# One transpose for both halves of the probabilities, and the gathers of the value sums moved to ScalarE's queue

## The reference

```python
xn = _layernorm(x)
q = (xn @ Wq)                       # 16 heads of 32
k, v = split(xn @ Wkv)              # 4 key/value heads of 32
scores = q k^T / sqrt(32) + alibi bias, causal mask
attn = softmax(scores)              # 2048 x 2048 per head
out = attn @ v                      # then @ Wo + bo
gate = xn @ Wg^T ; up = xn @ Wu^T   # 4096 wide, weights from 4-bit codes and block scales
inter = gelu(gate) * up
x + attention(xn) + inter @ Wd^T
```

## Time and profile before

| | |
|---|---|
| time, median of 3 runs | 1842.21 us (1841.89 to 1845.7) |
| the profiled execution | 1845.56 us, its span 1843.7 us |
| TensorE busy | 1495.3 us, 81% |
| VectorE busy | 1262.5 us, 68% |
| ScalarE busy | 996.4 us, 54% |
| GpSimd busy | 996.7 us, 54% |
| mean granted TensorE clock | 0.927 of full speed |
| DMA transposes of probabilities | 768 |
| gather DMAs | 256 |

### The profile page before, as it was taken

One profiled execution on the slowest core, in us unless ns is written; L12 is line 12 of the kernel. 1 busy time (PEld: TensorE's weight loads), 2 busy tenths in 40 slices (PEclk: granted clock), 3 DMA queues, 4 the chain that ended last, 5 costly groups with the idle time before them and its releaser, 6 DMA issues. The chain is left out here.

```text
span 1843.7 us, 29952 instructions
## 1 busy us (share of the span) xinstructions
PE 1495.3 (81%) x9281; PEld 718.2 (39%) x9281; DVE 1262.5 (68%) x2642; ACT 996.4 (54%) x2124; POOL 996.7 (54%) x670
## 2 busy tenths in 40 slices
PE   6868878778878889878878879888878888788669
PEld 5733434333333334333333434333333434333234
DVE  7747677676847677677847677576757677676556
ACT  3336556555655556555655556565645556565430
POOL 3116556475555656475545656475546556475331
PEclk9978989999899999999989999899988999998889
DMA  7777868686787768686777778685877768686766
GB/s 214 213 163 143 145 110 158 108 151 122 139 143 132 152 119 157 109 154 127 145 136 132 149 121 162 111 156 111 144 138 130 148 122 160 108 147 114 121 140 210
DMA packets 793655, 261.08 MB, mean 142 GB/s; under 512 B 745696, under 2 KB 762984, under 8 KB 792952
## 3 DMA queue, kind: packets, MB, share of 16 engines
q1 hardware_dynamic: 789176, 253.53, 72.6%
q10 hardware_dynamic: 4320, 5.64, 1.1%
HBM read 52.30 MB, written 21.89 MB: 40 GB/s over the span
## 5 line engine op out<-in xcount | busy, mean ns | idle before, releaser
L1703 POOL TENSOR_TENSOR plo<-p,phi 128x1024 f16<-128x1024 f32 (+7 forms) x384 | 614.6, 1608 | 639.7 <-DMA ptl<-plo 566.5
L1436 ACT ACTIVATE p<-s_ps,shift 128x512 f32<-128x512 f32 (+3 forms) x640 | 393.1, 619 | 226.0 <-DVE shift L1572 132.1
L1448 ACT ACTIVATE phi<-p 128x1024 f16<-128x1024 f32 (+7 forms) x384 | 308.7, 807 | 273.9 <-issue 186.8
L1330 PE MATMUL s_ps<-kst,qst 128*128 128x512 f32 (+3 forms) x640 | 360.6, 565 | 86.8 <-ACT p L1436 68.9
L1551 DVE TENSOR_REDUCE mxp<-s_ps 128x1 f32<-128x512 f32 x384 | 260.5, 682 | 144.1 <-PE s_ps L1330 143.4
L1355 PE MATMUL o_ps<-pth,vst 128*32 128x256 f16 (+1 forms) x2304 | 142.2, 313 | 204.2 <-DMA ptl<-plo 150.5
L1508 DVE TENSOR_TENSOR acc<-down_ps,acc 128x512 f32<-128x512 f32 x237 | 161.4, 681 | 95.9 <-PE down_ps L1291 94.6
L1291 PE MATMUL down_ps<-wh,ih 128*128 128x512 f16 x506 | 203.3, 402 | 24.8 <-DVE acc L1508 24.7
L1553 DVE CUSTOM_DVE_ANT_0 s_ps<-s_ps,mask_row 128x128 f32<-128x128 f32 (+3 forms) x256 | 126.3, 493 | 138.3 <-PE s_ps L1330 137.7
L1313 PE MATMUL gate_ps<-xh,wh 128*128 128x512 f16 x512 | 206.3, 403 | 0.0
L1355 PEld LDWEIGHTS o_ps<-pth,vst 128*32 128x32 f16 x2304 | 99.4, 109 | 267.5 <-issue 201.2
(11 more groups left out here) (262 smaller groups left out, 2260.8 us busy)
## 6 DMA issues: line engine op xcount, KB each, us to landing
o<-oraw SPq DMA_DIRECT2D x256, 64.0 KB, 2.0
qst<-q_parts SPq DMA_DIRECT2D x192, 64.0 KB
q_parts<-o SPq DMA_DIRECT2D x24, 256.0 KB, 3.4
pth<-phi SPq DMA_TRANSPOSE x384, 3.2
ptl<-plo SPq DMA_TRANSPOSE x384, 3.2
raw<-L_ffn_gate_W_packed_dram SPq DMA_DIRECT2D x16, 256.0 KB, 3.0
raw<-n_L_ffn_up_W_packed_dram SPq DMA_DIRECT2D x16, 256.0 KB, 3.1
raw<-L_ffn_down_W_packed_dram SPq DMA_DIRECT2D x32, 128.0 KB, 2.7
```

What stands on the lines that cost most here:

```text
L1330: nc.tensor.matmul(s_ring[n % len(s_ring)][:, 0:cols], qst[:, c, i4 * P:(i4 + 1) * P], kst[:, m * CH:m * CH + cols], start=True, stop=True ...
L1436: nc.scalar.activation(p32[p % PR][:, at:at + cols], s_ring[n % len(s_ring)][:, 0:cols], ACT.Exp, bias=shift[t % len(shift)][:, 0:1], accu ...
L1448: nc.scalar.activation(phi[n % PH][:, 0:cols], p32[n % PR][:, 0:cols], ACT.Copy).then_inc(phi_done, 1)
L1703: nc.gpsimd.tensor_tensor(plo[n % PH][:, 0:cols], p32[n % PR][:, 0:cols], phi[n % PH][:, 0:cols], ALU.subtract).then_inc(plo_done, 1)
```

## The change

The high and low part of a piece stand side by side in one buffer `pair` (up to 2048 columns), and one DMA transpose turns both into one ring `pt`, in which the low blocks of a part follow its high blocks. It stands where the low turn stood, two slots after the part. There are 24 such turns per head in place of 48. `pair` is a ring of `PH` = 3 buffers; `p32` a ring of `PR` = 2. `part_lo` no longer waits for a turn; `part_hi` waits only for the turn three parts before, no longer for `plo`; `exp` waits for `plo` two parts before. `values` waits for the turns of the last three parts, and reads the same blocks from `pt`, as many matmuls as before. The four gather DMAs are issued by ScalarE right behind its copy to `oraw`, with the waits that SP had, and a wait for the copy itself. Only the gather of head 1, chunk 0, stands later, in slot 13.

```diff
+def part_columns(p):
+    t, a = PARTS[p]
+    return min((t + 1) * P - 2 * CH * a, 2 * CH)
+
+def row_block(t, j, low):
+    a, count = j // (2 * TPC), part_columns(PARTS.index((t, j // (2 * TPC)))) // P
+    return 2 * ROOM[t] + 4 * TPC * a + j % (2 * TPC) + (count if low else 0)
...
-        put(tables.low_at, at + LOW_LAG, p)
+        put(tables.turn_at, at + TURN_LAG, p)
...
-GATHER_AT = {1: 3, 7: 0, 15: 1, 30: 2}
+LOAD_K_AT, LOAD_V_AT, LATE_GATHER_AT = 39, 0, 13
...
-        PR, PH = 3, 2
+        PR, PH = 2, 3
...
-        phi = [sb(f"phi{i}", [P, 2 * CH], F16) for i in range(PH)]
-        plo = [sb(f"plo{i}", [P, 2 * CH], F16) for i in range(PH)]
-        pth = sb("pth", [P, RING, P], F16)
-        ptl = sb("ptl", [P, RING, P], F16)
+        pair = [sb(f"pair{i}", [P, 4 * CH], F16) for i in range(PH)]
+        pt = sb("pt", [P, 2 * RING, P], F16)
...
-                    sp.wait_ge(done, n + 1 if done is phi_done else after(n + 1))
+                    sp.wait_ge(plo_done, after(n + 1))
...
-                    sp.dma_start_transpose(dst[:, at:at + count, :], rows[n % PH][:, 0:count * P]).then_inc(turned[n % PH], 16)
+                    sp.dma_start_transpose(pt[:, at:at + 2 * count, :], pair[n % PH][:, 0:2 * count * P]
+                                           ).then_inc(turned[n % PH], 16)
...
-                        for n in (last - 1, last):
-                            pe.wait_ge(hi_turned[n % PH], 16 * (n // PH + 1))
-                            pe.wait_ge(lo_turned[n % PH], 16 * (n // PH + 1))
+                        for n in range(max(last - PH + 1, 0), last + 1):
+                            pe.wait_ge(turned[n % PH], 16 * (n // PH + 1))
...
                         if n >= PH:
-                            act.wait_ge(hi_turned[n % PH], 16 * (n // PH))
-                            act.wait_ge(plo_done, after(n + 1 - PH))
-                        nc.scalar.activation(phi[n % PH][:, 0:cols], p32[n % PR][:, 0:cols], ACT.Copy).then_inc(phi_done, 1)
+                            act.wait_ge(turned[n % PH], 16 * (n // PH))
+                        nc.scalar.activation(pair[n % PH][:, 0:cols], p32[n % PR][:, 0:cols], ACT.Copy).then_inc(phi_done, 1)
...
                         nc.scalar.activation(oraw[:], o_ps[:], ACT.Copy).then_inc(oraw_done, 1)
+                        if (h, c) != (1, 0):
+                            gather_o(h, c)
+
+                    def gather_o(h, c):
+                        act.wait_ge(oraw_done, after(h * NCH + c + 1))
+                        if c == 0 and h >= 2:
+                            act.wait_ge(on_out, 32 * (h - 1))
+                        if c == 0 and h == 1:
+                            act.wait_ge(acc_done, after(NT))
+                        for part in range(VPARTS):
+                            act.dma_start(o3[h % 2][c * HD:(c + 1) * HD, part, :],
+                                          oraw[part * HD:(part + 1) * HD, :]).then_inc(o_out, 16)
...
                         pool.wait_ge(phi_done, n + 1)
-                        if n >= PH:
-                            pool.wait_ge(lo_turned[n % PH], 16 * (n // PH))
-                        nc.gpsimd.tensor_tensor(plo[n % PH][:, 0:cols], p32[n % PR][:, 0:cols], phi[n % PH][:, 0:cols],
-                                                ALU.subtract).then_inc(plo_done, 1)
+                        nc.gpsimd.tensor_tensor(pair[n % PH][:, cols:2 * cols], p32[n % PR][:, 0:cols],
+                                                pair[n % PH][:, 0:cols], ALU.subtract).then_inc(plo_done, 1)
```

More of the change, by code:

```diff
@@ L1014, in main_loop @@
         quarters = [xh[:, :, k * CH:(k + 1) * CH] for k in range(NCH)]
-        spare = [t[:].rearrange("p j n -> p (j n)")[:, 0:KVH * CH].rearrange("p (g n) -> p g n", g=KVH) for t in (pth, ptl)]
+        spare = [pt[:].rearrange("p j n -> p (j n)")[:, k * KVH * CH:(k + 1) * KVH * CH].rearrange("p (g n) -> p g n", g=KVH)
+                 for k in range(2)]
         whole = {0: quarters[0:2], 2: quarters[2:4], 3: spare}
@@ L1043, in main_loop @@
         values_done = sem("values_done")
-        hi_turned = [sem(f"hi_turned{i}") for i in range(PH)]
-        lo_turned = [sem(f"lo_turned{i}") for i in range(PH)]
+        turned = [sem(f"pair_turned{i}") for i in range(PH)]
         phi_done = sem("phi_done")
@@ L1156, in _, with turn @@
                 load_v(0)
-                def turn(h, p, done, rows, dst, turned):
+                def turn(h, p):
                     t, a = PARTS[p]
-                    n, count = h * NPART + p, min(t + 1 - 2 * TPC * a, 2 * TPC)
-                    sp.wait_ge(done, n + 1 if done is phi_done else after(n + 1))
+                    n, count = h * NPART + p, part_columns(p) // P
+                    sp.wait_ge(plo_done, after(n + 1))
                     before = [h * UNITS + u + 1 for u in units_in_room(t) if h * UNITS + u >= 0]
@@ L1165, in turn @@
                         sp.wait_ge(values_done, max(before))
-                    at = ROOM[t] + 2 * TPC * a
-                    sp.dma_start_transpose(dst[:, at:at + count, :], rows[n % PH][:, 0:count * P]).then_inc(turned[n % PH], 16)
+                    at = row_block(t, 2 * TPC * a, False)
+                    sp.dma_start_transpose(pt[:, at:at + 2 * count, :], pair[n % PH][:, 0:2 * count * P]
+                                           ).then_inc(turned[n % PH], 16)
                 def body(i, par, slots):
                     for s in slots:
-                        for h, p in items(PLAN.low_at, i, s):
-                            turn(h, p, plo_done, plo, ptl, lo_turned)
-                        for h, p in items(PLAN.part_at, i, s):
-                            turn(h, p, phi_done, phi, pth, hi_turned)
+                        for h, p in items(PLAN.turn_at, i, s):
+                            turn(h, p)
                         if i < 0 or s >= SLOTS:
@@ L1225, in first_raw @@
                         sp.dma_start(row, src.rearrange("(o n) -> o n", o=1).broadcast_to([P, C])).then_inc(bias_in, 16)
-                def gather_o(h, c):
-                    sp.wait_ge(oraw_done, after(h * NCH + c + 1))
-                    if c == 0 and h >= 2:
-                        sp.wait_ge(on_out, 32 * (h - 1))
-                    if c == 0 and h == 1:
-                        sp.wait_ge(acc_done, after(NT))
-                    for part in range(VPARTS):
-                        sp.dma_start(o3[h % 2][c * HD:(c + 1) * HD, part, :],
-                                     oraw[part * HD:(part + 1) * HD, :]).then_inc(o_out, 16)
                 def store_on(h):
@@ L1474, in body @@
                             o_copy(h, c)
+                        if i == 1 and s == LATE_GATHER_AT:
+                            gather_o(1, 0)
                 def wo_high(g):
```

31 lines of the change are left out of this document (11 added, 20 removed).

## The result

The changed kernel takes 1760.1 us (median of 4 runs, 1757.1 to 1760.5) against 1844.0 for the kernel before in the same rounds. The ratio is 0.954, 95% interval 0.951 to 0.956: 85 us faster by the ratio, where I forecast about 202. The direction was right; the time lies outside the range of 1598 to 1738.

A forecast was written before the change was run, and what follows sets the result against it. SP's DMA queue was taken as the bound. Per head 102.9 - 11.5 - 2.7 - 1.0 + 1.5 + 0.5 + 0.8 = 90.5 us; 14 heads -174, before them -22, last stretch -6: -202, so 1640 us, range 1598 to 1738.

The forecast's parts named there:

- wait for exponentials: TensorE waiting for exponentials that free a bank: of 4.1 us a head 2.7 goes, 1.4 stays from the row maximum.
- wait for turned blocks: TensorE waiting for turned blocks ahead of the value sums: all 11.5 us a head go.
- wait for keys and values: TensorE waiting for keys and values of a new group: the 1.9 us a head stay.
- TensorE's busy time (clock): TensorE's matmuls run slower for a while behind a wait; fewer stops give 1.0 us a head back.
- gathers, ring and coupling: Added per head: 1.5 us for ScalarE's gathers, 0.5 for p32 two deep, 0.8 for lateness SP hides between VectorE, ScalarE, TensorE.
- SP's queue sets the pace: SP's DMA issues stand back to back, 101 us of a 102.9 us head; the change takes them to about 61.
- That is hidden: A 16-block turn lands at about 4.2 us, hidden since value sums come four slots behind it, some 7.5 us.
- The issue of a wide turn: On SP's queue: 1.35 us per merged turn, on the line through one and eight blocks; ends 1.18 and 2.5.
- The rival of doubled cost: Turns beyond eight blocks take 2.5 us to issue on SP, about 80 us a head in all; 1678 us, chance 0.10.
- The ring of three `pair` buffers: `part_hi` waits for the turn three parts before; slower only if a part's round exceeds 12.9 us; chance 0.04, 1942 us.
- The floor of 86 us: Eight stretches of a head, each at its shortest, sum to 85.85 us; this change can't go far below.
- Coupling takes half of the gain: ScalarE, VectorE and TensorE hand work back and forth, or DMA engines answer later: head 96 us, 1725 us, chance 0.20.

The follow-up runs named there:

- f2: The kernel before, with the reciprocals' load and each of the two output stores cut into four DMAs; 25 us slower.
- g4: The changed kernel with each turn taking only the high blocks, 1 to 8 in place of 2 to 16, low blocks zero; 1696 us.
- e1: The changed kernel with the gathers issued by SP again in their old slots; 1746 us.
- e6: The changed kernel with three p32 buffers in place of two, gathers still on ScalarE; the buffer was worth nothing (0.9549 and 0.9536, intervals overlap).
- i1: The changed kernel with all five steps of VectorE's decoding of packed weights cut to a few columns; 34 us faster.
- i2: The changed kernel with gathers on SP, three p32 buffers, reciprocals' load in slot 14, stores in slot 44, and turns of high blocks only; ratio 0.8989.
- e7: The changed kernel with gathers back on SP in the old slots and three p32 buffers; 1735 us.
- f1: The changed kernel with the reciprocals' load and each of the two output stores cut into four DMAs; 17 us slower.

## Why the prediction was partly wrong

**The accounts.** Forecast per head 90.5, measured 97.6. TensorE's idle time and its clock explain the difference, from rows above and the earlier trace rows:

```
us a head                     before  forecast  measured  off by
wait for exponentials            4.1       4.2       8.7    +4.5
wait for turned blocks          11.5       0         3.2    +3.2
wait for keys and values         1.9       1.9       1.1    -0.8
TensorE's busy time (clock)     85.1      84.1      84.6    +0.5
```

(4.2 is the forecast's 1.4 that stays, and its 1.5, 0.5 and 0.8 for gathers, ring and coupling.) Together +7.4, against 97.6 - 90.5 = 7.1 measured; 14 heads make 99 us. Outside them the forecast was 28 us less and the spans give 14.5 less (402.8 to 388.3). 99 + 13.5 = 113 us, which is 1643.6 against 1755.3 + 1.9 for the profiled execution.

Two steps of the prediction failed. The larger, +4.5 us a head, is that the wait for exponentials would fall from 4.1 us; it rose to 8.7. The second, +3.2, is that the wait for turned blocks would go whole, as the wide turn's landing "is hidden".

**What bounds it.** "SP's queue sets the pace" was right for the kernel before: SP is idle there for 1.0 us a head, and f2, with 2.0 us more of SP's time a head, takes 1.9 us a head longer. Merging the turns alone saves 102 us, and 541.6 us of waits appear in SP's queue. But of the relief little came back: in the changed kernel SP has 28 us less to do a head, the head is 5.3 us shorter, and SP stands idle for 23.9.

**The second step that failed: landing.** The forecast said of it "That is hidden: the value sums come four slots behind the turn, some 7.5 us", and under TensorE's waits "The 11.5 us for turned blocks go". The landing itself was well sized (4.2 forecast, 4.5 measured). But a turn's time to TensorE is that of what stands ahead of it in the queue too: at the end of a head the two stores, behind which it is issued in 4.43 us and not in 1.96. In slots 42 to 47 the wait stayed, and that stretch takes 15.9 us as before. A narrow turn removes 4.0 us there, stores behind the turns 3.8, and with them the last turn lands after 4.3 us and not 6.3. I had looked at the plan's distance in slots and not at SP's stream at that place.

**The issue of a wide turn.** 1.35 us forecast, 1.96 measured for 16 blocks, inside the ends of 1.18 and 2.5. The line through one and eight blocks failed, and one of its two points was a fast case: the turn of the earlier trace rows took 1.18 us, but the 64 one-block turns of the kernel before have medians of 1.93 (high) and 1.22 us (low), against 1.25 for eight blocks. What stands ahead in the queue weighs as much as width there. The wide turns add up to 654 us over 14 heads, 46.7 a head, where 32.4 was forecast; those of g4 add up to 30.8. Two of the 24, behind the load and the stores, make 9.1 us of this. The rival of doubled cost was closer on the issue (1.96 of 2.5), and it too had SP with time to spare, as the trace has.

**The larger step that failed: the exponentials' wait.** It was to go from 4.1 to 1.4 before the additions, on the ground that its larger part came through `plo`, and that `plo` was late only because GpSimd stood for turns. But ScalarE's wait for GpSimd's low part did not go; it rose from 85.3 us to 109.1. GpSimd now waits for ScalarE's high part (392.4 us), ScalarE for GpSimd and, for 73.4 us, behind its own gathers. TensorE's waits for exponentials by slots say where this counts (my sums over 14 heads, us):

```
slots                     12-17   30-35   all
before                      0.7    10.8    57.9
after                      54.6    43.0   120.9
e1 (gathers on SP)         27.2    36.9    98.0
e6 (three p32 buffers)     50.9    42.2   123.3
i1 (no decoding)           49.3    39.2   105.0
```

In slots 12 to 17 of the changed kernel ScalarE's exponentials wait 67.6 us for GpSimd's low part (4.6 before). In e6 that wait is gone, but 67.7 us for VectorE's `shift` stand there instead, and the stretch stays at 14.3 us. In slots 30 to 35 they stand 41.4 us behind the gathers; with these on SP (e1), ScalarE waits 44.7 us for VectorE's step of the gelu there (10.6 in the changed kernel, 12.4 before), and the stretch takes 13.3 us. So where the runs take one wait away, the next one in the round between TensorE, VectorE, ScalarE and GpSimd stands in its place. Before, the two stretches had 11.5 us of TensorE's wait together; I take it that SP's lateness hid this round, which no run shows by itself. The runs name parts of the 8.7 us a head: gathers 1.7 (from 142.3 to 116.0 over some 15 heads, e1), VectorE's decoding 1.1 (i1), the ring of two nothing while the gathers are there (e6). What makes the rest is not settled; the order in which ScalarE and VectorE serve gelu, masks and exponentials is my guess, and I didn't change it.

**What came out as forecast.** The gathers' price: 1.5 us a head, 21 us, and e1 says 17. Their issues: 2.44 us for four. The ring of three `pair` buffers: `part_hi` waits 41.3 us for turns in 14 heads, and a part's round, from its rounding to the landing of its turn, takes 8.2 us by the median; three of 336 are over 12.9 us, the longest 14.6. The floor of 86 us: even i2, without half of the transposed data, takes 92.0 a head.

**The rivals.** "Coupling takes half of the gain" described what happened, with head 96 and 1725 us; its chance of 0.20 was too low and its price too small. My own 0.8 us a head for coupling was a bare guess, between a head where engines hid each other's lateness and stretches taken each at its best. "Wide turns cost double" foresaw a longer issue, but not that TensorE would lose more at the exponentials. i2 takes away what the runs found, width, gathers on ScalarE, ring and order, and reaches 0.8989, or 1656 us: only then is the forecast of 1640 in sight.

## What to carry to other kernels

When one queue is late everywhere, its relief is worth what the next dependency allows in each stretch, not the issue time that goes: read for each stretch what stands ahead of the last needed DMA in the same queue, and what the late engine was hiding between the others. Merging two transposes saves an issue but makes the transfer that someone waits for longer; put small stores and loads behind the last such transfer (36 us in e7, more than a third of what the merge gave), and then look at the first turn behind them: on the change itself the same move cost 17 us, since ScalarE waited for that one through the ring of three `pair` buffers. Issuing DMAs from a computing engine to free another queue paid here only while that queue was the bound: the same move gave 44 us before the merge and cost 17 after it.

## What the runs showed of the hardware

- A DMA transpose from SBUF to SBUF costs its queue 1.13 to 1.24 us for 1 to 8 blocks of 128 columns (medians in g4) and 1.5 to 2.0 us for 16; landing 2.3 us for 2 blocks, 4.5 for 16. It also depends on what runs beside and ahead of it: 8 blocks took 1.24 us in g4, 1.25 in the kernel before, and 1.72 among the wide turns of the changed kernel. The DMA share alone doesn't tell these apart: it is 0.53, 0.74 and 0.78.
- Behind a transfer with an outermost dimension of four, the issue of a 16-block turn took 4.43 us while the DMA share was 0.23, and it landed after 6.3. With the transfer cut into four it took 1.89 us and landed after 4.4 (f1, medians); a narrow turn in that place took 1.25 and 4.2 (g4).
- VectorE's multiplication by block scales (128x512) took 0.80 us on average in the kernel before and 1.07 after, with the same median; the rows of the two, before first:

```profile
L367 DVE TENSOR_TENSOR wf<-dec,sc 128x512 f32<-128x512 f16 x96 | 76.2, 796 | 0.1
```

```profile
L378 DVE TENSOR_TENSOR wf<-dec,sc 128x512 f32<-128x512 f16 x96 | 102.5, 1071 | 0.1
```

One of 1.81 us at 781.07 lay beside GpSimd's subtraction. That the overlap is the cause wasn't tested.
